# Attention and FFN on one core: weight pieces transposed by DMA as grid values and scaled after it

## The reference

```
def fp4_quant_dequant(x):                       # blocks of 16 along the last dim
    scale = max(abs(xb)) / 6.0                  # one per block
    xn = xb / scale
    q = _GRID[searchsorted(_MID, abs(xn))] * sign(xn) * scale
def fp4_linear(x, w):
    return einsum('bsk,nk->bsn', fp4_quant_dequant(x), fp4_quant_dequant(w))
x = x + attention(layernorm(x), ctx)
x = x + fp4_linear(silu(fp4_linear(xl, w_gate)) * fp4_linear(xl, w_up), w_down)   # xl = layernorm(x)
```

## Time and profile before

| | us |
|---|---|
| median of 3 runs | 1198.42 |
| lowest, highest | 1198.29, 1199.0 |
| the profiled execution | 1199.12 |
| its span, first to last instruction | 1196.7 |

### The profile page before, as it was taken

One profiled execution on the slowest core, in us unless ns is written; L12 is line 12 of the kernel. 1 busy time (PEld: TensorE's weight loads), 2 busy tenths in 40 slices (PEclk: granted clock), 3 DMA queues, 4 the chain that ended last, 5 costly groups with the idle time before them and its releaser, 6 DMA issues.

```text
span 1196.7 us, 21150 instructions
## 1 busy us (share of the span) xinstructions
PE 1172.7 (98%) x6874; PEld 1071.1 (90%) x6874; DVE 972.1 (81%) x1705; ACT 482.6 (40%) x1171; POOL 174.6 (15%) x305
## 2 busy tenths in 40 slices
PE   7899999999999999899999999999999999999998
PEld 6688888888888889799999999999999999999997
DVE  6778888878888876798888888888888888888865
ACT  3555656656556552333233233323323233322321
POOL 3433333323333310000000000000000000000000
PEclk9999999999999999899999999999999999999999
DMA  7112112112223227546545644644654564564461
GB/s 236 30 54 72 60 53 79 53 53 80 88 94 126 88 88 238 81 87 97 93 69 105 97 73 93 100 83 87 100 89 78 97 96 73 100 95 81 80 90 39
DMA packets 109381, 106.92 MB, mean 89 GB/s; under 512 B 70957, under 2 KB 81341, under 8 KB 109220
## 3 DMA queue, kind: packets, MB, share of 16 engines
q1 hardware_dynamic: 109348, 106.52, 42.9%
HBM read 66.60 MB, written 24.45 MB: 76 GB/s over the span
## 4 chain that ended last, share of the span: by engine, by line
PE 90%; DVE 4%; ACT 2%; DMA 1%; issue 1%; SPq 0%; POOL 0%; DVEq 0%; POOLq 0%; ACTq 0%
PE g_ps L175 7%; PE g_ps L176 7%; PE g_ps L177 7%; PE u_ps L176 7%; PE u_ps L175 7%; PE u_ps L177 7%; PE d_ps L1311 6%; PE d_ps L1312 6%; PE d_ps L1310 6%; PE o_ps L727 5%; PE s_ps L707 5%; PE s_ps L672 2%; PE w_ps L175 2%; PE w_ps L177 2%; PE w_ps L176 2%; PE q_ps L177 2%
## 5 line engine op out<-in xcount | busy, mean ns | idle before, releaser
L175 PE MATMUL g_ps<-wguh,xnh 128*128 128x352 f32 x512 | 168.5, 329 | 7.0 <-issue 5.6
L176 PE MATMUL g_ps<-wgul,xnh 128*128 128x352 f32 x512 | 165.7, 324 | 0.0
L177 PE MATMUL g_ps<-wguh,xnl 128*128 128x352 f32 x512 | 165.4, 323 | 0.0
L175 PE MATMUL u_ps<-wguh,xnh 128*128 128x352 f32 x512 | 165.2, 323 | 0.0
L176 PE MATMUL u_ps<-wgul,xnh 128*128 128x352 f32 x512 | 165.1, 322 | 0.0
L177 PE MATMUL u_ps<-wguh,xnl 128*128 128x352 f32 x512 | 164.8, 322 | 0.0
L830 ACT ACTIVATE probs<-s_ps,nsmax 128x77 f32<-128x77 f32 x512 | 114.1, 374 | 99.1 <-DVE nsmax L918 99.1
L1312 PE MATMUL d_ps<-wd,hql 128*128 128x512 f32 x330 | 128.9, 391 | 0.0
L1311 PE MATMUL d_ps<-wd,hqh 128*128 128x512 f32 x330 | 128.9, 391 | 0.0
L1310 PE MATMUL d_ps<-wd,hqh 128*128 128x512 f32 x330 | 128.4, 389 | 0.0
L1433 DVE TENSOR_TENSOR hid<-u_ps,silu 128x352 f32<-128x352 f32 x128 | 66.4, 519 | 48.5 <-PE u_ps L177 46.2
(11 more groups left out here) (151 smaller groups left out, 2517.0 us busy)
## 6 DMA issues: line engine op xcount, KB each, us to landing
scale_wide<-st_dram SPq DMA_DIRECT2D x248, 120.0 KB, 4.8
xin<-in_x_dram SPq DMA_DIRECT2D x32, 256.0 KB, 2.8
x_dram<-x SPq DMA_DIRECT2D x32, 256.0 KB, 2.0
xin<-x_dram SPq DMA_DIRECT2D x32, 256.0 KB, 2.7
out_dram<-y SPq DMA_DIRECT2D x32, 256.0 KB, 2.0
wd_dram<-wd_out SPq DMA_DIRECT2D x11, 512.0 KB, 3.8
wd<-wd_dram SPq DMA_DIRECT2D x1, 5632.0 KB, 17.4
w_in<-in_L_ffn_w_gate_dram SPq DMA_DIRECT2D x11, 256.0 KB, 2.9
```

Of the source, the lines that this page charges most:

```text
L175: pe.matmul(out, lh, rh, start=(i == 0), stop=False)
L176: pe.matmul(out, lh, rl, start=False, stop=False)
L177: last = pe.matmul(out, ll, rh, start=False, stop=(i == n - 1))
```

## The change

From piece 3 on (`BY_DMA`), 30 of the 33 pieces, the piece is no longer scaled and then transposed by TensorE. VectorE's last rounding step (`grid_values` in place of `take_magic`) writes the grid values as bf16 into `quant_magic`. SyncE issues a transposing DMA from there into `grid_t`. TensorE transposes only the 128 x 32 block scales (`transpose_scales`, one transpose in place of four), into `xn_ps`; ScalarE copies the 32 rows to SBUF (`scale_rows`, new, last of its iteration); SyncE stores them to HBM (`scales_out`) and loads them back by eight broadcast loads into `w_wide` (`scales_in`). GpSimd multiplies `grid_t` by `w_wide` into `w_q` (`scale_turned`) in place of `rescale_piece`, one iteration later. `piece_high` and `piece_low` then read `w_q` in SBUF in place of `xn_ps`, also one iteration later than before. The shift of a piece waits until the grid of the piece before it has been transposed, and TensorE's transpose of `xn` waits for the copied scale rows in place of the low half. SyncE's order is rewritten: load, scales out, scales in, store of a down piece, transposing DMA, then the store of `x1` and the load of `x`. The first FFN tile's input is rescaled into `quant_z`, as `w_q` still holds piece 32.

```diff
+BY_DMA = 3
     def rescale(self, dve, t):
         if reached(t):
             dve.wait_ge(self.xqT_done, t)
-        self.quant.rescale(dve, PIECES + t + 1, self.k.w_q[:]).then_inc(self.xq_ready, 1)
+        self.quant.rescale(dve, PIECES + t + 1, self.turned(t)).then_inc(self.xq_ready, 1)
...
+            def scales_out(n):
+                sp.wait_ge(w_rows_ready, n - BY_DMA + 1)
+                if n > BY_DMA:
+                    sp.wait_ge(w_wide_loaded, 16 * (P // BLK) * (n - BY_DMA))
+                sp.dma_start(ws_dram.rearrange("c b k -> (c b) k"), w_rows[:]).then_inc(w_rows_stored, 16)
+
+            def grid_transposed(n):
+                sp.wait_ge(wquant.grid_ready, n + 1)
+                if n > BY_DMA:
+                    sp.wait_ge(wq_ready, n)
+                sp.dma_start_transpose(grid_t[:], wquant.magic[:]).then_inc(grid_t_loaded, 16)
+
+            def scales_in(n):
+                sp.wait_ge(w_rows_stored, 16 * (n - BY_DMA + 1))
+                if n > BY_DMA:
+                    sp.wait_ge(wq_ready, n)
+                for b in range(P // BLK):
+                    sp.dma_start(w_wide[b * BLK:(b + 1) * BLK, :, :],
+                                 ws_dram[:, b, :].unsqueeze(0).to_broadcast([BLK, EC, P])).then_inc(w_wide_loaded, 16)
...
-            for t in range(T):
...
+            for a in range(1, T + 2):
+
+                n, t = a + 2, a - 2
+                if n + 1 < PIECES:
+                    load_piece(n + 1)
+                if by_dma(n - 1):
+                    scales_out(n - 1)
+                    scales_in(n - 1)
+                if GU_PIECES <= n - 2 < PIECES:
+                    store_piece(n - 2)
+                if by_dma(n):
+                    grid_transposed(n)
+                if t >= 0:
+                    store(t)
...
+            def scale_turned(n):
+                pool.wait_ge(grid_t_loaded, 16 * (n - BY_DMA + 1))
+                pool.wait_ge(w_wide_loaded, 16 * (P // BLK) * (n - BY_DMA + 1))
+                pool.wait_ge(wl_ready, n)
+                pool.tensor_tensor(w_q[:].rearrange("p (c k) -> p c k", k=P), grid_t[:], w_wide[:],
+                                   ALU.mult).then_inc(wq_ready, 1)
+
             def iteration(a, n, down=None):
                 if piece(n):
                     divide_piece(n)
-                    rescale_piece(n)
+                if by_dma(n - 1):
+                    scale_turned(n - 1)
...
+            def transpose_scales(n):
+                pe.wait_ge(wquant.scale_ready, n + 1)
+                pe.wait_ge(xnl_ready, min(n, T) if isinstance(n, int) else n)
+                pe.transpose(xn_ps[0:E // BLK, 0:P], wquant.scale[:], ident[:]).then_inc(w_rows_done, 1)
...
-                if not isinstance(t, int) or t >= 2:
-                    pe.wait_ge(wl_ready, t + 1 if not isinstance(t, int) else min(t + 1, PIECES))
-                elif t == 1:
-                    pe.wait_ge(wl_ready, 1)
+                if isinstance(t, int) and 1 <= t <= 2:
+                    pe.wait_ge(wl_ready, 2 * t - 1)
+                elif reached(t):
+                    pe.wait_ge(w_rows_ready, t - BY_DMA + 1)
...
-                if piece(n):
-                    transpose_piece(n)
+                if by_dma(n):
+                    transpose_scales(n)
                 if first_input(a, 0):
-                    pe.wait_ge(wl_ready, PIECES)
+                    pe.wait_ge(w_rows_ready, PIECES - BY_DMA)
+                    pe.wait_ge(xnl_ready, T)
                     f.transpose(pe, 0)
...
-                act.activation(dst, xn_ps[:].rearrange("p (c k) -> p c k", k=P), ACT.Copy).then_inc(wh_ready, 1)
+                src = w_q if by_dma(n) else xn_ps
+                act.activation(dst, src[:].rearrange("p (c k) -> p c k", k=P), ACT.Copy).then_inc(wh_ready, 1)
+
+            def scale_rows(n):
+                act.wait_ge(w_rows_done, n - BY_DMA + 1)
+                if not isinstance(n, int) or n > BY_DMA:
+                    act.wait_ge(w_rows_stored, 16 * (n - BY_DMA))
+                act.activation(w_rows[:], xn_ps[0:E // BLK, 0:P], ACT.Copy).then_inc(w_rows_ready, 1)
...
                 if piece(n):
+                    if not isinstance(n, int) or n > BY_DMA:
+                        act.wait_ge(grid_t_loaded, 16 * (n - BY_DMA))
                     wquant.shift(act, n + 1)
...
-                if piece(n):
-                    piece_high(n, down)
+                if by_dma(n - 1):
+                    piece_high(n - 1, down)
+                if by_dma(n):
+                    scale_rows(n)
...
+            def grid_values(n):
+                dve.wait_ge(wquant.sum_ready, n + 1)
+                dve.scalar_tensor_tensor(out=wquant.magic[:], in0=wquant.magic[:], scalar=ULP_FLOOR, in1=wquant.z[:],
+                                         op0=ALU.max, op1=ALU.subtract).then_inc(wquant.grid_ready, 1)
...
                 if piece(n):
+                    if not isinstance(n, int) or n > BY_DMA:
+                        dve.wait_ge(w_rows_done, n - BY_DMA)
                     wquant.block_scale(dve, n + 1)
...
-                    wquant.take_magic(dve, n + 1)
+                    grid_values(n)
...
-                if piece(n):
-                    piece_low(n, down)
+                if by_dma(n - 1):
+                    piece_low(n - 1, down)
```

More of the change, by code:

```diff
@@ L305, in rescale, with turned @@
             dve.wait_ge(self.xqT_done, t)
-        self.quant.rescale(dve, PIECES + t + 1, self.k.w_q[:]).then_inc(self.xq_ready, 1)
+        self.quant.rescale(dve, PIECES + t + 1, self.turned(t)).then_inc(self.xq_ready, 1)
+    def turned(self, t):
+        return self.quant.z[:] if t == 0 else self.k.w_q[:]
     def transpose(self, pe, t):
@@ L312, in transpose @@
         for c in range(EC):
-            last = pe.transpose(self.k.xn_ps[:, c * P:(c + 1) * P], self.k.w_q[:, c * P:(c + 1) * P], self.k.ident[:])
+            last = pe.transpose(self.k.xn_ps[:, c * P:(c + 1) * P], self.turned(t)[:, c * P:(c + 1) * P], self.k.ident[:])
         last.then_inc(self.xqT_done, 1)
@@ L328, with attention @@
 Over = namedtuple("Over", "q_done q_taken probsT_taken att_ready wo_done x1_ready xb_ready")
-def attention(nc, keep, k, f, x, ctx_in, Wq, bq, Wk, bk, Wv, bv, Wo, bo, w_gate, w_up, w_down, x1_dram, wd_dram):
+def attention(nc, keep, k, f, x, ctx_in, Wq, bq, Wk, bk, Wv, bv, Wo, bo, w_gate, w_up, w_down, x1_dram, wd_dram, ws_dram):
     with ExitStack() as ctx:
@@ L352, in attention @@
         w_in = sb("w_in", [P, 2, E])
+        grid_t = sb("grid_t", [P, EC, P], BF16)
+        w_rows, w_wide = sb("w_rows", [E // BLK, P]), sb("w_wide", [P, EC, P])
+        w_rows_done, w_rows_ready, w_rows_stored = sem("w_rows_done"), sem("w_rows_ready"), sem("w_rows_stored")
+        w_wide_loaded, grid_t_loaded = sem("w_wide_loaded"), sem("grid_t_loaded")
         x_loaded, piece_loaded, v_placed = sem("x_loaded"), sem("piece_loaded"), [sem(f"v_placed{b}") for b in range(B)]
@@ L428, in piece, with by_dma @@
             return not isinstance(n, int) or 0 <= n < PIECES
+        def by_dma(n):
+            return not isinstance(n, int) or BY_DMA <= n < PIECES
         def first_input(a, *tiles):
@@ L501, in sp_part @@
                                      vext[lo - h * CTX:hi - h * CTX, b, :, h, :]).then_inc(v_placed[b], 16)
-            for t in range(T):
[L504 to L514, removed]
+            for a in range(1, T + 2):
[11 more added lines that the diff above has]
+                    store(t)
+                    if t + RING < T:
+                        load(t + RING)
+                    else:
+                        f.load(sp, t + RING - T, x1_t[t + RING - T])
         def pool_part(pool):
@@ L646, in transpose_piece @@
                 pe.wait_ge(wq_ready, n + 1)
[L648 to L653, removed]
+                pe.wait_ge(xnl_ready, (1, 2, 2)[n])
+                if n == 2:
+                    pe.wait_ge(wl_ready, 2)
                 for c in range(4):
@@ L794, in piece_high @@
             def piece_high(n, down):
-                act.wait_ge(wT_done, n + 1)
+                if by_dma(n):
+                    act.wait_ge(wq_ready, n + 1)
+                else:
+                    act.wait_ge(wT_done, n + 1)
                 if down:
@@ L952, in piece_low @@
                     high, low = (w[:, :, bass.ds(n * P, P)] for w in (k.wguh, k.wgul))
-                dve.tensor_tensor(low, xn_ps[:].rearrange("p (c k) -> p c k", k=P), high.bitcast(F32),
+                src = w_q if by_dma(n) else xn_ps
+                dve.tensor_tensor(low, src[:].rearrange("p (c k) -> p c k", k=P), high.bitcast(F32),
                                   ALU.subtract).then_inc(wl_ready, 1)
+            def grid_values(n):
+                dve.wait_ge(wquant.sum_ready, n + 1)
+                dve.scalar_tensor_tensor(out=wquant.magic[:], in0=wquant.magic[:], scalar=ULP_FLOOR, in1=wquant.z[:],
```

(4 more changed lines are left out.)

13 lines of the change are left out of this document (9 added, 4 removed).

## The result

| | before | after |
|---|---|---|
| median, us | 1198.71 (1198.29 to 1199.34) | 1238.53 (1236.65 to 1241.07) |
| profiled execution | 1199.12 | 1236.65 |
| its span | 1196.7 | 1234.8 |
| start of the last `q` copy of the attention phase | 426.17 | 463.60 |

After to before is 1.0331 (1.0318 to 1.0343): 40 us slower, where 1.0 us less was forecast and 1203 was the upper end. Of the 38.1 us in the span 37.4 are there by the last `q` copy. The FFN phase is not touched.

The account below looks back on a forecast made before the run. A second loop over VectorE, GpSimd and ScalarE, 0.04 us behind TensorE, was taken to bound the kernel once TensorE gets shorter. 3.3 - 1.4 - 0.2 - 0.65 = 1.05, say 1.0 us gained: 1197.4 against the median, range 1190 to 1203.

Parts of the forecast that it names:

- The second loop as the bound: Attention loop: the once-per-iteration chain over VectorE, GpSimd and ScalarE, 0.04 us slack on TensorE, sets the pace after the change.
- TensorE, 0.33 per iteration: One scales' transpose replaces four in the attention loop: 0.33 us less per iteration, 9.9 us over 30 pieces.
- ScalarE's high half, +0.05: Reading w_q in SBUF instead of PSUM costs 0.05 us in the loop, 1.4 us over 27 iterations.
- Its copy of the scale rows, covered: ScalarE's new copy, 0.28 us (0.2 overlapped), is covered by 0.18 us against VectorE's path, costing nothing in the loop.
- VectorE's low half from SBUF and its grid values written as bf16: I take zero, bounded by 0.02 either way: Attention loop on VectorE: the new source and output format cost zero, within 0.02 us either way.
- GpSimd swaps its rescale ... Behind it on the queue stand the row scale and the bias: Same-size scaling (1.06 us) replaces the rescale, ends 8.6 us after low half's start, limit 10.96 for the row scale; cost zero.
- SyncE and the DMAs, zero: Scales out to HBM, eight broadcasts back and the transposing DMA land in time in the loop; costed at zero.
- The third rival: Scales land late: if broadcasts take over 4.9 us GpSimd delays each iteration; at 5.5, 14.5 us, so 1212; chance 0.08.
- The end of the phase, 0.65: Piece 32's high and low halves stand ahead of the first FFN tile's, adding 0.65 us before the first gate.
- The sum: 3.3 gained less 1.4, 0.2 and 0.65 gives 1.05, say 1.0 us gained from 9.9 taken off TensorE.
- 3.3 less 1.4: Attention phase: 3.3 us gainable from the second loop's slack, less 1.4 us for ScalarE's high half from SBUF.
- The rivals: TensorE's saving arrives, 1189.2, chance 0.22; ScalarE's copy becomes the path, 1201.4, 0.20; scales land late, 1212, 0.08.

Follow-up runs that it names:

- e3: The changed kernel with GpSimd's bias add moved one iteration later, behind the scaling, and the scaling waiting for the same iteration's grid values; 1210.54 us, 1.0103.
- e6: e3 with the first FFN tile's scalars ahead of GpSimd's last scaling; 1201.80 us, 1.0026.
- e14: e12 with the load of the x tile issued right behind the transposing DMA, once the residual has freed its slot; 1191.83 us, 0.9944.
- e10: e6 with ScalarE's copy of the scale rows made twice, the first into a scratch tile; 1201.32 us, 1.0018.
- e1: The changed kernel with GpSimd's bias add moved one iteration later, right behind the scaling of the piece; 1226.37 us, 1.0230.
- e7: The changed kernel with the first FFN tile's scalars ahead of the last scaling on GpSimd; 1227.51 us, 1.0241.
- e8: e5 with GpSimd's scaling waiting for the iteration's last nsmax, not for the grid values; 1195.32 us, 0.9971.
- e11: e8 with the eight broadcast loads issued for piece 3 alone, later pieces using piece 3's scales, so the weights are others; 1190.64 us, 0.9921.
- e5: The changed kernel with the low half moved into VectorE's next-iteration gap, scaling waiting for grid values, first FFN scalars ahead of the last scaling; 1197.83 us, 0.9990.
- e4: The kernel before with VectorE's low half reading w_q in SBUF from piece 3 on, and GpSimd's rescale waiting for it; 1209.08 us, 1.0092.
- e12: e8 with SyncE sending scale rows out and broadcasts in first, ahead of the store of x1 and the loads; 1197.98 us, 0.9992.

## Why the prediction was wrong, step by step

- *The second loop as the bound* held. With the two collisions off its path it runs at 12.52 to 12.57 (e3, e6; forecast 12.55 to 12.7), and TensorE's gain doesn't arrive. With the low half out of the loop it does: 12.32 in e14, 12.31 by the forecast's 0.33.
- *TensorE, 0.33 per iteration*, held: the scales' transpose shows 0.27 us with the next matmul 0.03 us behind its start (0.36 behind the first of the four before).
- *ScalarE's high half, +0.05*: 0.75 in place of 0.72. Held. *Its copy of the scale rows, covered*: held (e10, and no wait for `ath` in the changed kernel).
- *"VectorE's low half from SBUF and its grid values written as bf16: I take zero, bounded by 0.02 either way"* failed, by 1.03 and 0.38 us per iteration. The format does cost nothing (0.68 in e1), and so does the source while GpSimd is idle (0.69 in e1). What was missing is the neighbour. The bounds came from rows of VectorE alone, without asking what GpSimd runs at that moment. The row stands in the trace of before, GpSimd's timeline, 0.11 us behind the low half of the earlier trace rows (223.06), whose input in PSUM let both run at their own pace:

```profile
223.17 1.30 POOL L527 TENSOR_TENSOR xin<-xin,bo_all 128x512 f32 x1 [0.98 <-DVE xn L943]
```

- *"GpSimd swaps its rescale ... Behind it on the queue stand the row scale and the bias"*: the size held (1.17 for 1.06) and so did the times (it ends 7.7 us after the low half's start, forecast 8.6). But the swap also moves it beside the grid values, and for the last piece the queue behind it is another: `nmean`, not the row scale. That cost 8.3 us of standing still (8.4 by e7). The forecast listed who stands behind in the loop and didn't list it for the iteration in which the loop ends.
- *SyncE and the DMAs, zero*, held in the loops of the changed kernel: 1.4 us for the store and 1.9 for a broadcast to landing in the median, and no wait for `rstd`. At the end of the phase the way of the scales is what all stand still for, from the copy of piece 32's rows at 454.47 to the scaling at 461.59. And in e6 late scales decide which `nsmax` is hit, and in e8 they cost 4.7 us (e11), of which the order of e14 gives back some 3 (0.9971 to 0.9944). The third rival's mechanism is real, its place was wrong: it isn't what makes the changed kernel's loops slow.
- *The end of the phase, 0.65*: from the last `q` copy to the end of the span it is 0.7 us more than before, but that is luck. The first gate begins 14.58 us behind that copy in place of 12.72, and what follows it takes 1.2 us less than before in this execution. In the other versions of the changed kernel the first gate is 0.9 (e1, e3, e8) to 1.9 us further, or more (e5, 2.6), and not 0.65. So this term was too small too.
- *The sum, where the collisions are off the path.* That e6 without its six long iterations comes out at the forecast is part luck as well: up to the last `q` copy it would be 3.9 us ahead of the kernel before, where the forecast had 1.9 (3.3 less 1.4), and behind it it loses 1.9 in place of 0.65. 1.9 of the 3.9 lie in the first four iterations.
- *The rivals.* None was this one. The slower side was given 0.25, all by mechanisms that the runs rule out as the reason.

What stays open: why the first gate moves by 0.9 us in some versions and by 1.9 in others; e14 is 1.2 us above e11, which may be two chips or the loads; and which of the three large transfers delays the rows' store wasn't tried one by one.

## What to carry to other kernels

When an operand of a VectorE operation moves from PSUM to SBUF, or work on GpSimd moves in time, write down for each GpSimd operation what VectorE runs beside it, with the number of SBUF inputs of each, and price a collision at what is left of the operation that began first when the other one starts. Give the GpSimd operation a wait for a place that is safe rather than letting a DMA's landing choose it. For each queue that an edit touches, list who stands behind in the first and in the last iteration of a loop as well as in its middle.

## What the runs showed that was not expected

A held VectorE operation ends nearly as if it had begun only with the end of the GpSimd one: the low half 0.55 us after the bias add's end in the changed kernel (222.74, 222.19) and in e4 (370.55, 370.00), an `nsmax` 0.04 after it in e1 (213.05, 213.01), each its own length less some 0.13. So a short operation loses as much as a long one. An `nsmax` of 128 x 6 from SBUF, one input only, is held just like the wide operations: 1.10 us in place of 0.17 (e1). Row statistics with one wide SBUF input neither hold nor are held. In the changed kernel they take 0.69 us at 92.1, where the scaling had begun first, and here they begin first and the scaling takes its usual 1.17 (e14, start us, us, VectorE then GpSimd):

```profile
316.10 0.69 DVE L1004 BATCH_NORM_STATS2 stats<-xin 128x6 f32 x1
```

```profile
316.17 1.17 POOL L583 TENSOR_TENSOR w_q<-grid_t,w_wide 128x512 f32<-128x512 bf16 x1 [5.73 <-DVE nsmax L988]
```

How late the store of the scale rows, 16 KB, lands goes with what stands ahead of it on SyncE's queue. From its issue to that of the first broadcast it is, in the median of each trace: 1.4 us in the changed kernel and in e12, 2.4 in e14 (one load of 256 KB right ahead), 2.8 in e8 (three of 256 KB).
